# A graph layer and a routed feed-forward in one kernel: 38 blocks of routed rows pass both expert layers inside the edge gather, and the edge panels get narrower

## The chip, the cores and the metric

The kernel runs on one core of one Trainium2 chip. The metric is the device time of one execution in microseconds (us), lower is better. TensorE multiplies matrices, VectorE and ScalarE work element by element, GpSimd (POOL) here issues the gathers and scatters by indirect DMA, and SyncE (SP) issues the plain DMAs.

## The reference

```python
# _L0_gnn_ref, on mems = layernorm(x), 12500 nodes of 256 values, 200000 edges sorted by dst
mems2 = mems.at[yi].set(r[0])
_, nbr = jax.lax.top_k(-sum((mems2 - r)**2, -1), 7)         # 7 more edges into node yi
deg = segment_sum(w, col) + 2.0
dinv = rsqrt(deg)
xw = mems2 @ W
out = segment_sum((dinv[row] * w * dinv[col])[:, None] * xw[row], col)
out = out + (2.0 * dinv * dinv)[:, None] * xw
# _L0_ffn_ref, on x = layernorm(x1), 8 experts, D = 256, F = 1024
C = ceil(1.25 * T / E)                                      # T = 12500 rows, C = 1954
idx = argmax(softmax(x @ gate_w + gate_b))                  # one expert a row
pos = (cumsum(one_hot) * one_hot).sum(-1) - 1; kept = pos < C
hmid = relu(buf @ w1 + b1); ybuf = hmid @ w2 + b2           # buf: each expert's rows in order
y = nan_to_num(ybuf[idx, min(pos, C - 1)] * (prb * kept))
# the whole
x1 = x + _L0_gnn_ref(...); return x1 + _L0_ffn_ref(...)
```

dst is drawn as 12500 u^2, so that low nodes have many edges and high ones few.

## The kernel before

**Start.** VectorE derives from the edges' targets the degrees and, for each of 392 groups of 4 x 128 edges, the lowest target (`grp_base`). The scaled normalised rows are written to `z_table`. The aggregate `nodes` (256 x 12544, features on the partitions) stays in SBUF.

**Edge gather.** A turn is 8 groups (GS), and there are 49 turns, 0 to 48. For each group GpSimd issues four indirect DMAs of 128 rows of `z_table` (L561, in `gather_part`) into one of 8 slots; it may not be more than 8 groups ahead of TensorE (`agg_ps`). VectorE writes the group's one-hot panel, 4 tiles of 128 edges x 128 nodes (`select`, L1122). TensorE multiplies gathered rows and panel, 8 float32 matmuls that the trace shows as 16 records (`group`, L1645), where the gathered rows are the weights and the panel streams. VectorE adds the bank to `nodes` from the group's base on (`add_group`, L1132).

**Node blocks.** From turn Q0 = 26 on each turn also carries a block of four windows of 128 nodes that no later edge reaches: the convolution with W (`convolve`, L1672), the residual x1 (`residuals`), its norm (`variances`, `norms`, and `norm_step` on ScalarE), the transposes (L1683), the gate's logits (L1693, weights 128 x 128 and 8 columns), the softmax and choice of an expert (`gate_first`, `gate_second`), the rank among the expert's rows (`rank`, L1700 and L1701) and the row's place (`places`, from L1264). In the next turn GpSimd sends the four windows' rows (h, x1, token, gate) to their places in the DRAM table `xs` (`send`, L576). The last six windows follow after turn 48.

**Expert stage.** After the gather each of 8 experts has 8 steps of up to 256 rows (7 of 256 and one of 162). A step with no rows is skipped by an If on each engine. A step: SP loads the rows (4 slots), TensorE transposes them (L1777), VectorE copies them (L1456), TensorE makes up (L1795) and ScalarE the relu (L839), TensorE down (L1807); VectorE applies bias, gate and nan_to_num to two halves of 128 rows (L1488 to L1509), and GpSimd scatters each half into `out` (L674). For a skipped step VectorE still writes two lists of indices that point nowhere (L1516), and GpSimd still issues both scatters:

```python
dve.wait_ge(S["res_ok"], q * (2 * PC) + (2 * s + 2))
for slot in (s % 2 * 2, s % 2 * 2 + 1):
    slot_free(q, s, slot)
    nc.vector.memset(out_idx[:, slot:slot + 1], int(FAR)).then_inc(S["no_token"], 1)
```

Two experts are a pair and one pass of a loop; their weights (w1 and w2, 1 MB each an expert) lie in two buffers. Within an engine everything goes in program order, and the engines wait for each other by counting semaphores.

## Time and profile before

| | |
|---|---|
| median of 3 runs | 3101.61 us (3097.3 to 3101.98) |
| profiled execution: its time, its span | 3100.11 us, 3098.6 us |
| TensorE, VectorE, ScalarE, GpSimd busy | 2009.9, 1172.9, 457.6, 1850.6 us |
| first gather, last group of the gather ends | 172.1 us, 2293.9 us |
| first up of the expert stage | 2358.1 us |

Times are counted from the start of the span. An engine's busy time leaves out waits, branches and the issuing of DMAs by SP. A share over the whole span mixes the gather and the expert stage, and the two have different limits.

### The profile page before, as it was taken

What the parts mean: (1) busy time and instruction counts of PE and PEld (TensorE: products, weight loads), DVE (VectorE), ACT (ScalarE), POOL (GpSimd) and SP (SyncE); (2) the same over time, 40 slices, a digit from 0 to 9 for tenths busy, and PEclk for the clock granted to TensorE, in tenths of its full rate; (3) what the DMA queues carried; (4) which work ended last, traced back from release to release, by engine and by line L of the source; (5) the groups of instructions that cost most, each with busy time, mean ns of one, the idle gap of its engine ahead of it and who ended that gap; (6) DMA issues with size and microseconds to landing.
All of it is one profiled execution on the core that took longest, in us unless ns stands there. A gap on an engine that the chain in (4) does not pass through costs nothing. (4 is left out here: it accounts for less than half of the span.)

```text
span 3098.6 us, 38408 instructions
## 1 busy us (share of the span) xinstructions
PE 2009.9 (65%) x10840; PEld 1817.4 (59%) x10841; DVE 1172.9 (38%) x3705; ACT 457.6 (15%) x1152; POOL 1850.6 (60%) x1912
## 2 busy tenths in 40 slices
PE   2066555555566655666566666666655979989995
PEld 1045455555555555555555565565555868878875
DVE  8664222223212112343343343343332435434442
ACT  1341111000000000111111111111111212212221
POOL 6757777777777777777777777777741121111113
PEclk7577778777866677888887777777777989989997
DMA  9677555555444433444444444444442221222111
GB/s 234 177 223 204 154 148 146 150 150 144 142 123 130 131 104 105 130 131 138 143 130 137 143 133 134 137 129 128 136 123 97 69 77 49 68 88 78 57 59 33
DMA packets 229857, 388.32 MB, mean 125 GB/s; under 512 B 38937, under 2 KB 139967, under 8 KB 229546
## 3 DMA queue, kind: packets, MB, share of 16 engines
q0 software_dynamic: 92800, 245.57, 27.7%
q1 hardware_dynamic: 119274, 108.41, 11.8%
q10 hardware_dynamic: 17600, 32.15, 3.0%
q8 instruction: 85, 1.39, 0.2%
q14 instruction: 98, 0.80, 0.1%
HBM read 293.85 MB, written 100.43 MB: 127 GB/s over the span
## 5 line engine op out<-in xcount | busy, mean ns | idle before, releaser
L561 POOL DMA_INDIRECT arena<-z_table,arena x1568 | 1519.0, 969 | 497.5 <-issue 460.9
L1645 PE MATMUL bank<-arena 128*128 128x128 f32 x6272 | 1103.0, 349 | 805.9 <-issue 456.0
L1645 PEld LDWEIGHTS bank<-arena 128*128 128x128 f32 x6272 | 1029.8, 257 | 875.3 <-issue 609.7
L1132 DVE TENSOR_TENSOR nodes<-nodes,bank 128x256 f32 x392 | 165.1, 421 | 1336.1 <-PE bank L1645 1317.9
L674 POOL DMA_INDIRECT out<-arena x128 | 127.2, 994 | 630.1 <-DVE arena L1509 548.2
L1795 PE MATMUL bank<-arena 128*128 128x256 f32 (+1 forms) x1472 | 330.3, 384 | 24.4 <-issue 17.6
L1807 PE MATMUL bank<-arena 128*128 128x256 f32 (+1 forms) x1472 | 326.0, 379 | 0.0
L1795 PEld LDWEIGHTS bank<-arena 128*128 128x128 f32 x1472 | 282.7, 196 | 65.5 <-issue 26.9
L1807 PEld LDWEIGHTS bank<-arena 128*128 128x128 f32 (+1 forms) x1472 | 272.6, 187 | 40.1 <-issue 1.0
L1122 DVE TENSOR_TENSOR arena<-iota_b,arena 128x512 f32<-128x512 bf16 x392 | 268.6, 686 | 0.0
L839 ACT ACTIVATE arena<-bank,arena 128x256 f32<-128x256 f32 (+1 forms) x368 | 152.6, 466 | 560.2 <-PE bank L1795 560.2
L702 ACT ACTIVATE arena<-arena 128x16 int32<-128x16 int32 (+1 forms) x98 | 20.3, 210 | 790.9 <-PE bank L1645 789.9
L542 POOL DMA_INDIRECT arena<-dst_rows,first_i x98 | 100.0, 1021 | 47.4 <-issue 28.4
L576 POOL DMA_INDIRECT xs<-arena,send_idx x92 | 93.9, 1020 | 42.8 <-issue 26.5
L1456 DVE COPY arena<-bank 128x512 f32<-128x512 f32 (+1 forms) x46 | 31.2, 679 | 223.7 <-PE bank L1777 217.8
L1672 PE MATMUL bank<-arena,nodes 128*128 128x256 f32 x392 | 93.0, 391 | 0.0
L1488 DVE TENSOR_TENSOR arena<-bank,arena 128x256 f32<-128x256 f32 x92 | 39.0, 424 | 141.4 <-PE bank L1807 140.8
L745 ACT ACTIVATE arena<-arena,shift 128x256 f32<-128x256 f32 x98 | 49.1, 502 | 223.8 <-DVE arena L1139 177.5
L1672 PEld LDWEIGHTS bank<-arena,nodes 128*128 128x128 f32 x392 | 74.8, 196 | 9.5
L1590 PE MATMUL bank<-row_start,down_one 128*128 128x14 f32 (+3 forms) x10 | 3.1, 390 | 110.2 <-DVEq L934 110.2
L777 ACT ACTIVATE norm<-var 128x4 f32<-128x4 f32 (+1 forms) x24 | 4.9, 205 | 455.9 <-DVEq L1214 398.2
L1777 PE MATMUL bank<-ident,arena 128*128 128x128 f32 (+1 forms) x184 | 30.7, 288 | 57.1 <-DVEq L1529 28.2
(274 smaller groups left out, 1383.7 us busy)
## 6 DMA issues: line engine op xcount, KB each, us to landing
xs<-zeros ACTq DMA_DIRECT2D x122, 257.0 KB
arena<-z_table,arena POOLq DMA_INDIRECT x1568
arena<-xs SPq DMA_DIRECT2D x43, 514.0 KB, 4.0
arena<-in_L_ffn_w SPq DMA_DIRECT2D x16, 1024.0 KB, 7.6
arena<-in_x SPq DMA_DIRECT2D x98, 128.0 KB, 2.7
arena<-in_x SPq DMA_DIRECT2D x24, 512.0 KB, 4.2
out<-arena SPq DMA_DIRECT2D x24, 512.0 KB
nodes<-in_x SPq DMA_DIRECT2D x12, 896.0 KB, 11.9
```

The lines of the kernel that those rows point to most:

```text
L542: nc.gpsimd.indirect_dma_start(first_rows[:, h % 2, i, :], None, dst_rows, bass.IndirectOffsetOnAxis(ap=first_i[:, h * U + i:h * U + i + 1 ...
L561: nc.gpsimd.indirect_dma_start(gath[:, slot, t, :], None, z_table, bass.IndirectOffsetOnAxis(ap=idx_ring[:, half, s * GT + t:s * GT + t + ...
L576: nc.gpsimd.indirect_dma_start(xs, bass.IndirectOffsetOnAxis(ap=send_idx[:, i, s:s + 1], axis=0), h_send[:, i * BW + s, :], None, bounds_c ...
L674: nc.gpsimd.indirect_dma_start(out, bass.IndirectOffsetOnAxis(ap=out_idx[0:n, slot:slot + 1], axis=0), o_tile[0:n, slot, :], None, bounds_ ...
L745: nc.scalar.activation(sq[:, j, :], sq[:, j, :], ACT.Square, bias=shift[:, bass.ds(w, 1)], accum_out=dist[:, bass.ds(w, 1)]).then_inc(S["d ...
L839: nc.scalar.activation(hid[:, f, 0:n], up_bank[f // 2][:, f % 2 * CR:f % 2 * CR + n], ACT.Relu, bias=b1_pair[:, j * FT + f:j * FT + f + 1] ...
L1122: nc.vector.tensor_tensor(sel[:, j, :, :], iota_b[:, :].unsqueeze(1).to_broadcast([P, GT, P]), rel_b[:, bass.ds(g * GT, GT)].unsqueeze(2). ...
L1132: nc.vector.tensor_tensor(where, where, agg_bank[j][:, 0:D].rearrange("p (k c) -> p k c", k=KD), ALU.add).then_inc(S["agg_added"], 1)
L1645: last = nc.tensor.matmul(agg_bank[j][:, k * P:(k + 1) * P], gath[:, slot, t, k * P:(k + 1) * P], sel[:, j, t, :], start=(t == 0), stop=(t ...
L1672: last = nc.tensor.matmul(conv_out(j), nodes[:, k, (q - Q0) * BW + j, :], gnnw_sb[:, k, :], start=(k == 0), stop=(k == KD - 1))
L1795: last = nc.tensor.matmul(up_bank[b][:, i * CR:i * CR + n], w1_sb[:, j, k, f * P:(f + 1) * P], xs_feat[:, s % 2, k, 0:n], start=(k == 0), ...
L1807: last = nc.tensor.matmul(bank[4 + t][0:m, 0:D], hid[:, f, t * P:t * P + m], w2_sb[:, j, f, :], start=(f == 0), stop=(f == FT - 1))
```

## The change

- The node blocks begin at turn TS = 20. `TURN_OF` gives each of 23 its turn: 20 to 25, 27, 29, 31, 32, 34, 35, 37 to 40, 42 to 48. The last six windows still come after turn 48.
- From turn JT = 30 to 48 each turn carries two jobs, 38 in all. `choose` on VectorE picks, one turn ahead, the expert with the most placed rows that are not yet given out (30 small operations, 14 for each of two jobs and two more); a job with fewer than 256 rows to take works on rows of zeros behind the table. A job is a whole block: rows and weights loaded by SP, transposes, up, relu, down, results, and two scatters into `out`. It has one buffer for w1 and one for w2, in the first 32 windows of `nodes`, which are no longer needed by then.
- The expert stage keeps its 64 steps; `need_i` says which are left. Each engine reads that flag for every step, in place of the count for every pair.
- The panels are 64 nodes wide before turn 20 and 96 from there on. Three banks serve the groups from turn 20 on, four before.
- xs is zeroed by three DMAs a step instead of two, done by turn 20. Some small tensors share one block of SBUF. The way for unsorted edges (not taken with these inputs) is rebuilt to match.

```diff
+    NARROW, WIDE = 64, 96
+    WIDE_FROM = 160
+    WIDTHS = [(0, WIDE_FROM, NARROW), (WIDE_FROM, GROUPS, WIDE)]
...
-    Q0 = 26
+    TURNS = GROUPS // GS
+    TS = 20
     BW = 4
-    NB = GROUPS // GS - Q0
+    NB = 23
+    TURN_OF = []
+    for b in range(NB):
+        TURN_OF.append(max(TURN_OF[-1] + 1 if b else TS, math.ceil((GROUPS * math.sqrt((b + 1) * BW / NW) + 3) / GS)))
...
+    JT = 30
+    NJ = 2 * (TURNS - JT)
...
+        wide_bank = [bank[0], bank[1], bank[6]]
+        job_up = [bank[7], bank[5]]
...
+            def second_weights(turn):
+                k = 2 * (turn - JT)
+                e = sp.value_load(job_i[0:1, turn % 2, 1, 0:1], min_val=0, max_val=NE - 1)
+                up_done(k)
+                load_job_w1(e)
+                down_done(k)
+                load_job_w2(e, 1)
+
+            def next_first(turn):
+                k = 2 * (turn - JT)
+                sp.wait_ge(S["job_ok"], turn + 1 - JT + 1)
+                e, row = job_regs(turn + 1, 0)
+                if k >= 0:
+                    sp.wait_ge(S["res_ok"], 2 * (k + 1))
+                load_job_rows(0, row)
+                if k >= 0:
+                    up_done(k + 1)
+                load_job_w1(e)
+                if k >= 0:
+                    down_done(k + 1)
+                load_job_w2(e, 0)
...
+            for t in range(TS, TURNS):
+                if t >= JT:
+                    second_rows(t)
+                if t in BATCH_AT:
+                    store_x1(BATCH_AT[t])
+                if t >= JT:
+                    second_weights(t)
+                if t - 1 in BATCH_AT:
+                    b = BATCH_AT[t - 1]
+                    sp.wait_ge(S[f"sent{b % 2}"], 16 * BW * (b // 2 + 1))
+                    if b + 2 <= NB:
+                        load_x(b + 2)
+                if t == JT - 1:
+                    sp.wait_ge(S["conv_ps"], 32)
+                if JT <= t + 1 < TURNS:
+                    next_first(t)
...
+            def scatter_job(turn, i):
+                k = 2 * (turn - JT) + i
+                for h in range(2):
+                    pool.wait_ge(S["res_ok"], 2 * k + h + 1)
+                    nc.gpsimd.indirect_dma_start(
+                        out, bass.IndirectOffsetOnAxis(ap=out_idx[:, 2 * i + h:2 * i + h + 1], axis=0), job_out[:, 2 * i + h, :], None,
+                        bounds_check=last_node, oob_is_err=False).then_inc(S[f"out_done{2 * i + h}"], 16)
...
+                    def between(s):
+                        if t > JT and h == 0 and s == 2:
+                            scatter_job(t - 1, 0)
+                        if t > JT and h == 1 and s == 0:
+                            scatter_job(t - 1, 1)
+                        if t - 1 in BATCH_AT and h == 1 and s == 2:
+                            send(BATCH_AT[t - 1] + 1, BATCH_AT[t - 1] % 2)
...
+            def select(g, j, width=NARROW):
+                nc.vector.tensor_tensor(panel(j, width), iota_b[:, 0:width].unsqueeze(1).to_broadcast([P, GT, width]),
+                                        rel_b[:, bass.ds(g * GT, GT)].unsqueeze(2).to_broadcast([P, GT, width]),
...
+            def choose(turn):
+                then(nc.vector.tensor_scalar(count[:, :], taken_f[0:1, :], float(FULL_ROWS), None, ALU.min))
+                for i in range(2):
+                    then(nc.vector.tensor_tensor(avail[:, :], count[:, :], given[:, :], ALU.subtract))
+                    then(nc.vector.tensor_reduce(e_max[:, :], avail[:, :], AX.X, ALU.max))
...
+            def job_features(turn, i):
+                k = 2 * (turn - JT) + i
+                dve.wait_ge(S["xT_ps"], k + 1)
+                if k:
+                    dve.wait_ge(S["l1_ps"], FB2 * k)
+                nc.vector.tensor_copy(job_feat, bank[5].rearrange("p (k c) -> p k c", k=KD)).then_inc(S["xT_ok"], 1)
...
+            def job_results(turn, i):
+                k = 2 * (turn - JT) + i
+                dve.wait_ge(S["l2_ps"], 2 * k + 2)
+                for h in range(2):
+                    slot = 2 * i + h
+                    if turn > JT:
+                        dve.wait_ge(S[f"out_done{slot}"], 16 * (turn - JT))
+                    nc.vector.tensor_tensor(job_out[:, slot, :], bank[4][:, h * D:(h + 1) * D], job_b2[:, i, :], ALU.add).then_inc(S["y_ok"], 1)
+                dve.wait_ge(S["y_ok"], 2 * k + 2)
+                tokens = job_rows[:, i, :, TOK]
+                slots = slice(2 * i, 2 * i + 2)
+                then(nc.vector.tensor_scalar(out_miss[:, slots], tokens, 0.0, FAR, ALU.is_equal, ALU.mult))
+                then(nc.vector.scalar_tensor_tensor(out_f[:, slots], tokens, -1.0, out_miss[:, slots], ALU.add, ALU.add))
+                then(nc.vector.tensor_copy(out_idx[:, slots], out_f[:, slots]))
+                for h in range(2):
+                    y = job_out[:, 2 * i + h, :]
+                    token = job_rows[:, i, h, :]
+                    then(nc.vector.tensor_scalar(y, y, token[:, GATE:GATE + 1], None, ALU.mult))
+                    nc.vector.tensor_scalar(job_low, y, -BIG, -1.0e4, ALU.is_lt, ALU.mult).then_inc(S["dve_ch"], 1)
+                    nc.vector.tensor_scalar(job_high, y, BIG, 1.0e4, ALU.is_gt, ALU.mult).then_inc(S["dve_ch"], 1)
+                    ch[0] += 2
+                    then(nc.vector.tensor_scalar(job_fin, y, 0.0, 0.0, ALU.mult, ALU.is_equal))
+                    then(nc.vector.tensor_tensor(job_high, job_high, job_low, ALU.add))
+                    then(nc.vector.copy_predicated(job_high, job_fin, y))
+                    nc.vector.tensor_tensor(y, token[:, D:2 * D], job_high, ALU.add).then_inc(S["res_ok"], 1)
+                    dve.wait_ge(S["res_ok"], 2 * k + h + 1)
...
+                    g = t * GS + i
+                    add_group(g, i % SR, False, WIDE)
+                    if g + SR < GROUPS:
+                        select(g + SR, i % SR, WIDE)
+                    if i == 0 and t > JT:
+                        job_results(t - 1, 1)
                     if i == 1:
-                        if b:
-                            places(b - 1, BW)
-                        residuals(b, BW)
-                    if i == 2:
+                        if t >= JT:
+                            job_features(t, 0)
+                        if t - 1 in BATCH_AT:
+                            places(BATCH_AT[t - 1], BW)
+                        if JT <= t + 1 < TURNS:
+                            choose(t + 1)
+                        if b is not None:
+                            residuals(b, BW)
+                    if i == 2 and b is not None:
                         variances(b, BW)
-                    if i == 3:
+                    if i == 3 and b is not None:
                         norms(b, BW)
-                    if i == 6:
+                    if i == 4 and t >= JT:
+                        job_results(t, 0)
+                    if i == 5 and t >= JT:
+                        job_features(t, 1)
+                    if i == 6 and b is not None:
                         gate_first(b, BW)
-                    if i == 7:
+                    if i == 7 and b is not None:
                         gate_second(b, BW)
...
+                with dve.If(need(dve, q, s) > 0):
...
+            def turn_job(turn, i):
+                k = 2 * (turn - JT) + i
+                pe.wait_ge(S[f"xs_in{i}"], 16 * (turn - JT + 1))
+                if k:
+                    pe.wait_ge(S["hid_ok"], FT * k)
...
+            def up_job(turn, i):
+                k = 2 * (turn - JT) + i
+                pe.wait_ge(S["xT_ok"], k + 1)
+                pe.wait_ge(S["w_in0"], 16 * (k + 1))
+                for c in range(FB2):
+                    if c >= 2:
+                        pe.wait_ge(S["hid_ok"], FT * k + 2 * (c - 1))
+                    for h in range(2):
+                        f = 2 * c + h
+                        for kk in range(KD):
+                            last = nc.tensor.matmul(job_up[c % 2][:, h * CR:(h + 1) * CR], job_w1[:, kk, f * P:(f + 1) * P],
+                                                    job_feat[:, kk, :], start=(kk == 0), stop=(kk == KD - 1))
+                    last.then_inc(S["l1_ps"], 1)
...
+            def down_job(turn, i, placed):
+                k = 2 * (turn - JT) + i
+                pe.wait_ge(S["w_in1"], 32 * (k + 1))
+                pe.wait_ge(S["cnt_ok"], placed)
+                if k:
+                    pe.wait_ge(S["y_ok"], 2 * k)
...
+                        if t - 1 in BATCH_AT:
+                            rank(BATCH_AT[t - 1], BW, 2 * max(t - JT, 0))
+                        if b is not None:
+                            convolve(b, BW)
+                        if t >= JT:
+                            turn_job(t, 0)
+                    if slot == 2 and t >= JT:
+                        up_job(t, 0)
+                    if slot == 3 and t >= JT:
+                        down_job(t, 0, placed)
                     if slot == 4:
-                        turn_rows(q, i, BW, first)
-                    if slot == 5:
-                        logits(q, BW)
-            for q in range(Q0, Q0 + NB):
-                slot_turn(q, (q - Q0) % 2, q == Q0)
-            last_q = Q0 + NB
-            rank(last_q - 1, (NB - 1) % 2, BW)
-            convolve(last_q, TW)
-            turn_rows(last_q, NB % 2, TW)
-            logits(last_q, TW)
-            rank(last_q, NB % 2, TW)
+                        if b is not None:
+                            turn_rows(b, BW)
+                        if t >= JT:
+                            turn_job(t, 1)
+                    if slot == 5 and b is not None:
+                        logits(b, BW)
+                    if slot == 6 and t >= JT:
+                        up_job(t, 1)
+                    if slot == 7 and t >= JT:
+                        down_job(t, 1, placed)
```

## Rows read from the trace of the kernel before

**Rows 1.** Page, parts 1 and 2: busy us by engine; granted TensorE clock in 40 slices.

```profile
PE 2009.9 (65%) x10840; PEld 1817.4 (59%) x10841; DVE 1172.9 (38%) x3705; ACT 457.6 (15%) x1152; POOL 1850.6 (60%) x1912
...
PEclk7577778777866677888887777777777989989997
```

**Rows 2.** Groups by line: busy us, mean ns of one, idle before.

```profile
L561 POOL DMA_INDIRECT arena<-z_table,arena x1568 | 1519.0, 969 | 497.5 <-issue 460.9 <-DMA z_table<-nodes 19.8 <-PE bank L1645 13.4
...
L1795 PE MATMUL bank<-arena 128*128 128x256 f32 (+1 forms) x1472 | 330.3, 384 | 24.4 <-issue 17.6 <-DVE arena L1456 6.8
...
L674 POOL DMA_INDIRECT out<-arena x128 | 127.2, 994 | 630.1 <-DVE arena L1509 548.2 <-issue 71.0 <-DVEq L1520 10.9
```

**Rows 3.** Windows: us, busy by engine (instructions), granted clock, DMA share, GB/s.

```profile
1410.00:2294.00 884.00, 558.46 (x3289) 524.72 (x3288) 346.90 (x1256) 126.75 (x265) 668.15 (x685) 0.78 0.45 134
...
2358.00:3098.60 740.60, 666.00 (x3124) 577.01 (x3124) 317.14 (x1185) 153.29 (x371) 127.18 (x128) 0.94 0.20 63
```

**Rows 4.** Timeline, GpSimd: the first gather of turns 20, 26, 30 and 48.

```profile
989.78 1.32 POOL L561 DMA_INDIRECT arena<-z_table,arena  x1 [0.30 <-issue]
...
1232.19 0.95 POOL L561 DMA_INDIRECT arena<-z_table,arena  x1 [0.31 <-issue]
...
1410.64 0.94 POOL L561 DMA_INDIRECT arena<-z_table,arena  x1 [0.30 <-issue]
...
2241.08 0.94 POOL L561 DMA_INDIRECT arena<-z_table,arena  x1 [0.30 <-issue]
```

**Rows 5.** Timeline, TensorE: turn 30's first group and the last group.

```profile
1417.28 3.49 PE L1645 MATMUL bank<-arena 128*128 128x128 f32 x16 [3.02 <-issue]
...
2290.72 3.15 PE L1645 MATMUL bank<-arena 128*128 128x128 f32 x16 [2.61 <-issue]
```

**Rows 6.** Timeline, TensorE: groups of 128 columns and logits of 8 columns.

```profile
1722.73 0.96 PE L1693 MATMUL bank<-arena 128*128 128x8 f32 x8
...
1730.86 3.75 PE L1645 MATMUL bank<-arena 128*128 128x128 f32 x16 [6.28 <-issue]
...
1735.75 2.02 PE L1645 MATMUL bank<-arena 128*128 128x128 f32 x16 [1.13 <-issue]
...
2315.26 1.85 PE L1693 MATMUL bank<-arena 128*128 128x8 f32 x8 [0.47 <-ACT r_y L793]
```

**Rows 7.** Chain that ended last, in order of time: an expert's first blocks.

```profile
3030.06 9.83 PE bank L1795 x32
...
3040.33 6.91 PE bank L1807 x32
3047.24 6.91 PE bank L1795 x32
3054.15 0.44 PE bank L1777 x4
```

**Rows 8.** Timeline, VectorE: first and last operation of half a block's results.

```profile
2602.47 0.42 DVE L1488 TENSOR_TENSOR arena<-bank,arena 128x256 f32<-128x256 f32 x1
...
2605.53 0.42 DVE L1509 TENSOR_TENSOR arena<-arena 128x256 f32<-128x256 f32 x1
```

**Rows 9.** Timeline, VectorE: places, residuals, variances and norms of a node block.

```profile
1704.55 0.18 DVE L1264 TENSOR_TENSOR arena<-arena,bank 128x32 f32<-128x32 f32 x1
...
1707.50 1.66 DVE L1199 SCALAR_TENSOR_TENSOR arena<-bank,dinv,arena 128x256 f32<-128x256 f32 x4 [0.23 <-DVE arena L1277]
...
1710.01 1.40 DVE L1206 BATCH_NORM_STATS2 arena<-arena 128x6 f32<-128x256 f32 x4
...
1712.44 0.23 DVE L1213 SCALAR_TENSOR_TENSOR var<-gap,var 128x4 f32<-128x4 f32 x1
```

**Rows 10.** DMA issues: KB each, median us to landing.

```profile
arena<-in_L_ffn_w SPq DMA_DIRECT2D x16, 1024.0 KB, 7.6
...
nodes<-in_x SPq DMA_DIRECT2D x12, 896.0 KB, 11.9
```

**Rows 11.** Timeline, TensorE around skipped steps; GpSimd's last scatter.

```profile
2496.42 7.07 PE L1795 MATMUL bank<-arena 128*128 128x256 f32 x32
...
2528.18 2.07 PE L1795 MATMUL bank<-arena 128*128 128x256 f32 x4 [6.92 <-issue]
...
3093.67 1.10 POOL L674 DMA_INDIRECT out<-arena  x1 [0.30 <-issue]
```

More of the change, by code:

```diff
@@ L1 @@
+import math
 import concourse.bass as bass
@@ L1730, in _ @@
             with pe.If(n_bad > 0):
-                pe.wait_ge(S["rep_bad"], 1)
-                nc.tensor.matmul(bank[4][:, 0:GROUPS], ones[0:1, :], grp_bad[0:1, :], start=True, stop=True).then_inc(S["rep_dst"], 1)
+                with pe.Fori(0, NW) as w:
+                    pe.wait_ge(S["gp_in"], w * 16 + 16)
+                    for k in range(KD):
+                        last = nc.tensor.transpose(turned(0)[:, k, :], h_send[:, 0, D + k * P:D + (k + 1) * P], ident[:, :])
+                    last.then_inc(S["gp_pe"], 1)
+                pe.wait_ge(S["gp_free"], NW + 1)
                 pe.sem_inc(S["rep_free"], 1)
```

613 lines of the change are left out of this document (376 added, 237 removed).

## Prediction, made before the changed kernel ran

> **What bounds the kernel now.** I read the page first [rows 1]. TensorE is busy for 65% of the span, and its granted clock stands near 0.75 of full until about slice 29 and near 0.95 after it: two stages. The groups by line say what they are [rows 2]: 1568 row gathers on GpSimd (L561), later 1472+1472 matmuls of the expert layers, 32 and 32 a block of 256 rows, so 46 blocks. The windows [rows 3] give the sizes. From 1410 to 2294 GpSimd works 668 of 884 us and, with 0.30 us between two issues, never rests, while TensorE has 37% to spare. From 2358 to the end TensorE works 666 of 741 us. So the gather stage is bound by GpSimd's issuing, the expert stage by TensorE, and the change moves work from the second into the spare time of the first.
>
> GpSimd's turn of 8 groups comes from starts of its turns [rows 4]: turn 20 at 989.78 and 26 at 1232.19 give 40.4 us without sends; 30 at 1410.64 and 48 at 2241.08 give 46.1 us with four sends. The first matmul of turn 30 starts at 1417.28, the last group's at 2290.72 [rows 5].
>
> **What TensorE needs in such a turn.** A group is 16 records. At full clock (2.4 GHz) it takes 2.02 us, which is 0.111 us each and 1.8 us from one group to the next; at the half clock 3.75 us, or 3.4 from one to the next [rows 6]. The narrow panels shorten the streamed operand from 128 columns to 96 (64 before turn 20). The gate's matmuls with 8 columns show what that is worth: 8 records take 0.96 us at full and 1.85 us at half clock, again about 0.112 and 0.21 us each. A record with a weight load of 128 columns has this floor, so I book nothing for the narrow panels on TensorE; before turn 20 GpSimd hides TensorE anyway. The Trainium skill ("TensorE: Matmul & The Clock Gate", Back-to-back issue gap) gives for an isolated matmul a gap that falls with the columns, and says that this counts too little where weights are loaded; by the first half of it a group would take 1.3 us and not 1.8.
>
> A block costs 6.91 us up and 6.91 down plus 0.44 of transposes, 14.26 us in all [rows 7]. Two blocks and eight groups are 28.5+14.4 = 42.9 us; a node block's convolution (16 records of 0.216), transposes, logits (16 of 0.112) and ranks add some 7. That is 50 us at full clock in a turn with a node block, against GpSimd's 46.1 + 4 scatters of 1.29 (0.99 busy [rows 2] + 0.30) = 51.3. Neither alone gives the turn: the engines wait for each other in it.
>
> **The turn's chain.** VectorE does a new job's results between two groups. A half block takes 3.48 us today [rows 8]; without the small steps that are now shared, 2.65, so two halves with their bias adds are 6.7 us. The 13 small operations of places, most of them chained, take from 1704.55 to the residuals at 1707.50 [rows 9]: 0.2 us each, so the 30 of choose are 6.0 us, and places with one more 3.3. With the select at 96 columns (0.55) and the add (0.34), time 0 at the start of the turn's group 0:
> - add 0 at 2.2, select, two bias adds: y_ok at 4.1. Only then TensorE goes on with rank (0.7), convolution (3.5), transposes (0.5); group 1 starts at 8.8.
> - add 1 at 11.0, select, job_features 0.7: up(0) starts at 12.7, group 3, down(0), group 4 starts at 28.3.
> - Meanwhile VectorE: places, choose, residuals until 23.7, variances, norms until 29.5 (their lengths from [rows 9]: residuals 1.66, variances 2.7; norms are six small ones, 1.3); ScalarE's four norms end at 31.8, the node transposes 32.1, group 5 from 32.6, logits, group 6 until 38.0.
> - add 4 at 30.5, results 6.7, add 5, features: up(1) at 39.9 instead of 38.0; group 7, down(1): 55.5.
>
> So the turn is 55.5 us with a node block (15 of the 19 turns) and some 54.2 without (30, 33, 36, 41), if the clock stays full. It will not quite. TensorE has three waits of 2 to 5 us, and [rows 7] shows what follows a wait: the first up after one takes 9.83 us, 2.9 more than 6.91. Group 4 to group 6 is thin work (8-column logits and transposes between waits); I take half clock in a part of it (+1.3) and of the next up (+2), and +1.4 for the start of the turn: 60.2. The turns without node blocks wait 5 us before each up: 59.5. Ends: 55.5 with no loss; 68 with all eight groups at half clock (8 x 1.6).
>
> **The parts.**
> 1. Start: 13 more small chained VectorE operations on the bases; 0 to 4 us, taken 2. Later zeroing of xs in threes lies on ScalarE's queue behind the gather: nothing.
> 2. Turns 20 to 29: seven of them now carry sends (21 to 26, 28), before three (27 to 29): four more. 7 x 46.1 + 3 x 40.5 - (1410.64 - 989.78) = +23.
> 3. Turns 30 to 48: 15 x 60.2 + 4 x 59.5 = 1141, against 2293.9 - 1417.3 = 876.6: +264.5. Covers: GpSimd has 51 us of issuing in 60; its scatter of the second block waits until VectorE is 10 us into the next turn, which leaves it four gathered groups ahead, some 5 us of slack. SP's queue: rows, x1 store, then w1 of the second block, which must follow the store (x1_ok at 23.7) though up(0) ended at 19.6; needed at 39.9, so 15 us to land. 1 MB takes 7.6 us in the quiet stage and 0.9 MB 11.9 us at the crowded start [rows 10]; DMA would go from 134 GB/s [rows 3] to about 12 MB a turn, 200 GB/s. Taken as hidden. The other loads have 17 us or more.
> 4. Between the stages: 64 us stay; job_results ahead of places costs some 1.5.
> 5. Expert stage. I worked out the routing from the reference's inputs and followed choose(): of the 38 jobs 34 find a full block, 4 run empty; 12 of 46 blocks remain (three of them 162 rows), and 52 of 64 steps are skipped, before 18. A skip is not free: SP, TensorE and VectorE step through it, and GpSimd still issues two scatters, at least 2.6 us. Last up of an expert at 2496.42, next up at 2528.18 [rows 11]: less 14.26+3.1 for the block up to its last result, four skips and a pair's end took 14.4, 3.6 each. After the last block's result (3061.5+17.4 = 3078.9) five skips last until the end at 3098.6, 3.9 each. I take 3.0, bounds 2.6 and 3.9. Sum: 12 x 14.26 less 3 x 2.5 = 164; 8 runs of blocks, each with 3.1 to drain and 2.9 slow start = 48; 52 x 3.0 = 156; 368 in place of 744: -376. Each expert still takes 35 us or more, so its 2 MB of weights stay hidden.
>
> Sum: 2 + 23 + 264.5 + 1.5 - 376 = -85: span 3098.6 to 3013.6. The profiled execution took 3100.1, the median of the runs is 3101.6, so I add 1.5: **3015 us**, 2.8% less.
>
> **Rivals.** A measurement of this kernel tells about 0.2% (6 us) from no change.
> - Forecast, turns of 57 to 63 us: 0.42.
> - The clock stays up, turns of 55.5: 3015 - 19 x 4.7 = 2926. For it: in the expert stage clock 0.94 with shorter waits. 0.15.
> - Streamed columns count: a group would fall by 0.45 us, 3.6 a turn, 2948. This is the Trainium skill's isolated gap; the 8-column records speak against it. 0.03.
> - GpSimd is the bound (51.3): 2846. Needs chains shorter than I count. 0.05.
> - Slower: the half clock holds through all groups, turns of 68. Place: groups 4 to 7 and 0 to 2, between up and down. Price 12.8 a turn over 55.5, time 3163. For it: the granted clock is 0.78 in 1410 to 2294 [rows 3], though TensorE works 63%. Against: up and down are dense. It decides from turns of 64.7 us on (3101.6 - 3015 = 87 over 19 turns). 0.15.
> - w1 of the second block lands 5 us late, after 20 us: up(1) waits, turns of 65, 3106. For: twice the traffic. 0.15, half of it over the bound.
> - Skips at 3.9: 3062. 0.05.
>
> Slower by over 0.2%: 0.15 + half of 0.15, less what lands within: 0.20. Within 0.2%: 0.05. Faster: 0.75. Range 2920 to 3125: both clock cases' near ends and the late weights are in it; about 0.1 lies beyond each end.
>
> **What would show it.** Turn length: group 0 of turns 30 and 48 about 60 us apart each turn; 55 means no clock loss, 51 GpSimd, 65 or more a late weight load (TensorE waits for in_L_ffn_w) or half clock (groups of 3.7 us). Spacing in 96-column groups 0.112 at full clock. Turn 30 starts 25 us later than before. 12 blocks and 52 skips in about 370 us. The prediction falls if the turn is misjudged by 5 us, since 19 turns multiply it.

## The result and the profile after

The changed kernel takes 2986.17 us (median of 4 runs, 2983.49 to 2990.36); the kernel before took 3101.12 beside it. The ratio is 0.963 (95% interval 0.962 to 0.965): 3.7% faster. The forecast was 3015 us, 2.8% faster. The profiled execution has a span of 2986.1 us, 112.5 less than before.

The page, parts 1, 2 and 5, of the changed kernel:

```profile
PE 2166.6 (73%) x11158; PEld 1972.3 (66%) x11159; DVE 1186.5 (40%) x4294; ACT 477.1 (16%) x1222; POOL 1919.0 (64%) x1988
...
PEclk7575555555555666665899999998999999686777
...
L694 POOL DMA_INDIRECT arena<-z_table,arena x1568 | 1510.6, 963 | 497.3 <-issue 489.4
...
L1998 PE MATMUL bank<-arena,nodes 128*128 128x256 f32 x1216 | 310.6, 419 | 46.4 <-DVE arena L1498 46.1
...
L830 POOL DMA_INDIRECT out<-arena,early_block x128 | 126.8, 991 | 270.9 <-DVE arena L1780 153.6
```

Beside [rows 1, 2]: TensorE does the same expert work in another place. The granted clock is near full in slices 20 to 34, where the gathers and the blocks now run together, and falls in the last stage, where there is little left to do. It is also lower than before in the turns ahead of them; the section on the panel widths comes back to that. The windows of turns 30 to 48 and of the last stage (columns as in [rows 3]; the second begins 5.4 us ahead of that stage's first matmul):

```profile
1431.00:2541.00 1110.00, 997.45 (x5707) 898.30 (x5707) 614.64 (x2362) 234.88 (x558) 722.64 (x736) 0.92 0.63 198
2602.00:2986.10 384.10, 188.40 (x816) 155.55 (x816) 87.30 (x402) 39.02 (x99) 126.78 (x128) 0.74 0.19 57
```

In the turns TensorE works 90% of the time, where it had 63% in [rows 3]; GpSimd, which never rested before, now works 65%. The bound has passed from GpSimd to TensorE and its waits. Cut at the same places as the prediction's parts (the expert stage from TensorE's first transposes, at 2354.9 us before and 2607.4 after):

| part | before, us | after, us | change | predicted |
|---|---|---|---|---|
| up to GpSimd's first gather | 172.1 | 174.6 | +2.5 | +2 |
| turns 0 to 19 (GpSimd) | 817.7 | 806.7 | -11.0 | 0 |
| turns 20 to 29 (GpSimd) | 420.9 | 441.3 | +20.4 | +23 |
| GpSimd's turn 30 to TensorE's | 6.6 | 8.4 | +1.8 | 0 |
| turns 30 to 48 (TensorE) | 876.6 | 1110.5 | +233.9 | +264.5 |
| between the stages | 61.0 | 65.9 | +4.9 | +1.5 |
| expert stage | 743.7 | 378.7 | -365.0 | -376 |

One turn of the middle stage, TensorE's timeline (start, length, line, tiles, count, idle time before and its releaser), from the first group of turn 37 to the first of turn 38:

```profile
1837.70 1.92 PE L1916 MATMUL bank<-arena 128*128 128x96 f32 x16
1839.46 3.65 PE L1943 MATMUL bank<-arena,nodes 128*128 128x256 f32 x16
...
1843.38 3.71 PE L1916 MATMUL bank<-arena 128*128 128x96 f32 x32
1849.29 8.86 PE L1998 MATMUL bank<-arena,nodes 128*128 128x256 f32 x32 [2.20 <-DVE arena L1498]
1857.98 1.92 PE L1916 MATMUL bank<-arena 128*128 128x96 f32 x16
1859.74 7.10 PE L2012 MATMUL bank<-nodes,early_block 128*128 128x256 f32 x32
...
1873.24 2.48 PE L1916 MATMUL bank<-arena 128*128 128x96 f32 x16
1878.31 8.70 PE L1998 MATMUL bank<-arena,nodes 128*128 128x256 f32 x32 [2.59 <-DVE arena L1498]
1886.85 1.92 PE L1916 MATMUL bank<-arena 128*128 128x96 f32 x16
1888.60 7.10 PE L2012 MATMUL bank<-nodes,early_block 128*128 128x256 f32 x32
1895.54 1.92 PE L1916 MATMUL bank<-arena 128*128 128x96 f32 x16
```

This is the chain of the forecast. A group of 96 columns takes 1.92 us at full clock, the 128-column one 2.02 [rows 6]: at full clock the streamed columns are nearly free. Both ups of this turn wait 2 us or more for VectorE's features (L1498; 18 of the stage's 38 ups do) and take 8.7 to 8.9 us instead of 7.1, and the group ahead of the second (group 6, at 1873.24) takes 2.48; each down is full speed. The turn is 57.8 us; all turns lie between 55.7 and 60.5.

What the engines waited for in that stage (engine, tile and line, releaser: us, times, longest):

```profile
POOL out L719 <- DVE nodes L1526: 151.0, 33, 11.9
...
PE bank L1998 <- DVE arena L1498: 46.1, 18, 4.3
```

GpSimd stands 151 us ahead of the scatters of a block. There is no wait of TensorE for the weights of a block.

### The profile page after: what moved, and what is told of

The parts are those of the page before. It is cut to its first block and busy times, and to the rows that moved or that the text cites. A ratio compares the mean times of both kernels' runs of the same rounds, so it can differ in the third digit from the quotient of the medians.

```text
span 2986.1 us, 40946 instructions
## 1 busy us (share of the span) xinstructions
PE 2166.6 (73%) x11158; PEld 1972.3 (66%) x11159; DVE 1186.5 (40%) x4294; ACT 477.1 (16%) x1222; POOL 1919.0 (64%) x1988
## 5 line engine op out<-in xcount | busy, mean ns | idle before, releaser
L1916 PE MATMUL bank<-arena 128*128 128x96 f32 (+1 forms) x6272 | 1133.7, 359 | 340.4 <-issue 147.9
L1916 PEld LDWEIGHTS bank<-arena 128*128 128x128 f32 x6272 | 1096.8, 271 | 376.6 <-issue 212.0
L1316 DVE TENSOR_TENSOR nodes<-nodes,bank 128x192 f32 (+1 forms) x392 | 128.1, 327 | 1302.7 <-PE bank L1916 1255.7
L1998 PE MATMUL bank<-arena,nodes 128*128 128x256 f32 x1216 | 310.6, 419 | 46.4 <-DVE arena L1498 46.1
L1998 PEld LDWEIGHTS bank<-arena,nodes 128*128 128x128 f32 x1216 | 255.4, 213 | 91.7 <-DVE arena L1498 49.5
L2012 PE MATMUL bank<-nodes,early_block 128*128 128x256 f32 x1216 | 269.8, 380 | 0.0
L2012 PEld LDWEIGHTS bank<-nodes,early_block 128*128 128x128 f32 x1216 | 228.1, 190 | 29.4
L967 ACT ACTIVATE early_block<-bank,early_block 128x256 f32<-128x256 f32 x304 | 127.2, 469 | 587.3 <-PE bank L1998 587.1
L1305 DVE TENSOR_TENSOR arena<-iota_b,arena 128x384 f32<-128x384 bf16 (+1 forms) x392 | 195.5, 499 | 0.4 <-issue 0.3
L1943 PE MATMUL bank<-arena,nodes 128*128 128x256 f32 x392 | 110.9, 446 | 0.0
L2121 PE MATMUL bank<-arena 128*128 128x256 f32 (+1 forms) x384 | 93.9, 411 | 20.9 <-DVE arena L1729 20.9
L2121 PEld LDWEIGHTS bank<-arena 128*128 128x128 f32 x384 | 79.4, 222 | 35.0 <-issue 23.8
L1943 PEld LDWEIGHTS bank<-arena,nodes 128*128 128x128 f32 x392 | 88.0, 231 | 14.7
```

The source lines that it names most:

```text
L967: nc.scalar.activation(job_hid[:, f, :], job_up[f // 2 % 2][:, f % 2 * CR:(f % 2 + 1) * CR], ACT.Relu, bias=job_b1[:, i, f:f + 1]).then_in ...
L1305: nc.vector.tensor_tensor(panel(j, width), iota_b[:, 0:width].unsqueeze(1).to_broadcast([P, GT, width]), rel_b[:, bass.ds(g * GT, GT)].uns ...
L1316: nc.vector.tensor_tensor(where, where, held[:, 0:KD * width].rearrange("p (k c) -> p k c", k=KD), ALU.add).then_inc(S["agg_added"], 1)
L1916: last = nc.tensor.matmul(held[:, k * width:(k + 1) * width], gath[:, slot, t, k * P:(k + 1) * P], panel(j, width)[:, t, :], start=(t == 0 ...
L1943: last = nc.tensor.matmul(conv_out(j), nodes[:, k, b * BW + j, :], gnnw_sb[:, k, :], start=(k == 0), stop=(k == KD - 1))
L1998: last = nc.tensor.matmul(job_up[c % 2][:, h * CR:(h + 1) * CR], job_w1[:, kk, f * P:(f + 1) * P], job_feat[:, kk, :], start=(kk == 0), st ...
```

## The experiments

They were run on several chips of the same type, and these were of two kinds. On one kind, where the result was taken too, the kernel before takes 3101 us, on the other (three chips) 3850 to 3854; below they are the fast and the slow kind. Times are therefore compared only with kernels of the same kind, and where the kinds differ it is said. The table has them all; the segments are from the profiled executions, turns by TensorE's groups, the last stage from its first up (turns 30 to 48 here end with the last group, 7 us before the last down).

| kernel | kernel before there | time | ratio to before (95%) | turns 0-19 | 20-29 | 30-48 | last stage |
|---|---|---|---|---|---|---|---|
| before_again | 3100.7 | 3099.2 | 1.000 (0.999-1.001) | 794.9 | 421.7 | 877.1 | 739.9 |
| changed kernel | 3101.1 | 2986.2 | 0.963 (0.962-0.965) | 781.9 | 443.1 | 1103.6 | 375.6 |
| e7_panels_128 | 3100.7 | 3013.4 | 0.973 (0.971-0.975) | 783.7 | 446.8 | 1114.7 | 376.4 |
| e1_no_jobs | 3854.4 | 3815.1 | 0.989 (0.987-0.991) | 923.7 | 633.3 | 1185.1 | 745.9 |
| e2_jobs_from_40 | 3854.4 | 3793.8 | 0.983 (0.981-0.986) | 928.1 | 636.9 | 1354.0 | 554.8 |
| e3_start_panels_128 | 3854.4 | 3834.6 | 0.993 (0.990-0.996) | 934.3 | 620.3 | 1572.8 | 379.7 |
| e4_free_skips | 3854.4 | 3841.4 | 0.997 (0.995-1.000) | 935.7 | 629.6 | 1545.4 | 381.0 |
| after_again | 3852.7 | 3841.2 | 0.998 (0.996-0.999) | 922.1 | 629.9 | 1569.3 | 381.7 |
| e5_scatter_later | 3852.7 | 3760.8 | 0.976 (0.973-0.979) | 925.2 | 628.6 | 1492.2 | 379.6 |
| e9_one_look | 3852.7 | 3829.4 | 0.993 (0.990-0.995) | 942.7 | 619.1 | 1579.4 | 354.7 |
| e10_all | 3852.7 | 3714.0 | 0.963 (0.960-0.966) | 921.2 | 630.9 | 1468.7 | 351.3 |
| e10b_all | 3850.2 | 3712.7 | 0.965 (0.962-0.968) | 930.8 | 618.2 | 1470.9 | 351.3 |
| e3b_start_panels_128 | 3850.2 | 3843.5 | 0.997 (0.996-0.999) | 928.6 | 633.2 | 1572.1 | 377.3 |

**The same change on the slower kind of chip.** after_again is the changed kernel.

> The changed kernel itself, on the chip of this group of runs. If that is the chip on which the kernel before took 3854 us, every theory expects 3840 +- 15 us, as with free skips (3841) and with 128-column panels at the start (3835), since neither of these two edits showed an effect beyond 0.5%; a time below 3790 there would mean that both of them cost 50 us, and they would have to be read anew. If it is a chip on which the kernel before takes 3101 us, all expect 2986 +- 5.

3841.2 us, as expected: there the change is worth 0.25% (0.07 to 0.43), not 3.7%. before_again was to show where the kinds part.

> The kernel before itself, profiled on the chip of this run. If it is the chip on which it took 3852 us: theory A, that chip is slower where TensorE works beside GpSimd's row gathers and nowhere else, expects turns 0 to 19 at 920 to 935 us as in every kernel run there (818 on the first chip), turns 20 to 29 at 620 to 640 (421), turns 30 to 48 at 1185 to 1225, which is 310 to 350 more than the 876.6 of the first chip, and the stage from the first expert block to the end at 744 to 750 as on the first (743.7). Rival B, the chip is slower everywhere by the same share (24%), expects 920 us for that last stage. If it is a chip like the first, the profile's segments repeat within 1%.

It ran on the faster kind and repeated the first profile within 3 us in every segment, so its theories were not put to the test; the other kernels answer. The last stage takes 745.9 us without jobs on the slow kind (e1) and 739.9 on the fast, 381.7 and 375.6 with them: rival B, slower everywhere by the same share, has fallen. Turns 0 to 19 take 922 instead of 782 us, turns 30 to 48 1569 instead of 1104. So nearly all of the slow kind's loss lies where TensorE works beside the gathers; the start is longer too (188.5 instead of 174.6 us up to the first gather), the last stage by 6. TensorE's timeline in turn 39 of after_again shows how:

```profile
2557.38 2.81 PE L2012 MATMUL bank<-nodes,early_block 128*128 128x256 f32 x11
2561.24 0.46 PE L2012 MATMUL bank<-nodes,early_block 128*128 128x256 f32 x1 [1.05 <-issue]
...
2573.94 0.58 PE L2012 MATMUL bank<-nodes,early_block 128*128 128x256 f32 x1 [1.51 <-issue]
2576.04 0.58 PE L2012 MATMUL bank<-nodes,early_block 128*128 128x256 f32 x1 [1.52 <-issue]
2578.15 0.59 PE L2012 MATMUL bank<-nodes,early_block 128*128 128x256 f32 x1 [1.52 <-issue]
2580.94 0.58 PE L2012 MATMUL bank<-nodes,early_block 128*128 128x256 f32 x1 [2.21 <-issue]
...
2589.54 2.67 PE L1916 MATMUL bank<-arena 128*128 128x96 f32 x16
```

and the windows of two stretches of that turn:

```profile
2560.00:2584.00 24.00, 7.58 (x14) 3.92 (x14) 2.15 (x10) 2.33 (x4) 17.76 (x19) 0.58 0.56 185
2588.00:2600.00 12.00, 11.59 (x81) 10.98 (x79) 7.99 (x28) 3.57 (x10) 1.21 (x2) 0.78 0.47 154
```

One down (L2012) takes 32 us instead of 7.1, its matmuls starting 1.4, 2.1 or 2.8 us apart and waiting for nothing that the profile shows. In the first window GpSimd works 17.8 of 24 us and TensorE gets 14 matmuls done; in the second GpSimd rests and TensorE does 81 in 12 us. Spacings of that sort (over 0.65 us from one matmul's start to the next's, the next waiting for nothing) sum to 752 us in after_again, where the span is 853 us longer than on the fast kind, and to 1.6 us in the profiles of the fast kind. They do not come in every stretch in which GpSimd issues, but all of them save 1.6 us start within 6.4 us behind the start of an issue of GpSimd. GpSimd issues for most of the gather, so that this nearness alone proves little. Their cause is not settled.

**How much of it is the blocks' move, and what it is worth per block.** e1 sets `JT = 49` (no block moved; what follows the last turn for such blocks goes too), e2 `JT = 40`:

```
-    JT = 30
+    JT = 49        # e2: 40
```

> The changed kernel without its 38 jobs: panels of 64 and 96 and node blocks from turn 20 on stay, all 46 blocks pass in the expert stage. Theory (the gain is the jobs' alone: blocks leave the expert stage at 14.26 us less the price of a skip, and lengthen the turns 30 to 48): the expert stage goes back to about 743 us, turns 30 to 48 to 46.1 with sends and 40.3 without, 853 in all in place of 1110; 3088 us, 0.3 to 0.6% under the kernel before. Rival (the narrow panels bring a good part of the 3.7%): 3050 us or less.

> Jobs in turns 40 to 48 alone, 18 in place of 38, all with a full block. Theory (each turn with two jobs costs 13.5 us more than one without, each block moved saves 14.26 less 3.15 for its skip): 3088 + 9 x 13.5 - 18 x 11.1 + 9 = 3018 us. Rival (a job turn is long because of its start-up and its waits once, so fewer turns are cheaper in proportion, or the late turns with their node blocks are the dear ones): 3000 or less, or 3035 or more.

Both ran on the slow kind. The absolute numbers that were expected belong to the fast kind and stay untested. The last stage can be read, since the kinds agree on it: 46 blocks take 745.9 us, 28 take 554.8 and 12 take 381.7, counted by the matmuls of the ups (32 each). A block moved away is worth 191.1/18 = 10.6 us and 173.1/16 = 10.8: the trade is linear, and a block's 14.26 us [rows 7] are not all saved, 3.5 of them stay, as the price of the step that skips it and its share of the breaks between blocks. The other side of the trade is the turn. On the slow kind ten turns with jobs (30 to 39) take 808.4 us and without them 606.6, 20.2 more a turn; the 16 blocks that these turns take out of the last stage give back 17.3. On the fast kind the same ten turns went from 458.8 (before_again) to 582.6, 12.4 a turn. The two are not like for like: the kernel before has a node block and its sends in each of these turns, the changed one in seven of ten. Seven turns of 46.1 and three of 40.4 us [rows 4] make 444, if GpSimd bounded them; by this estimate the blocks themselves cost 13.9 a turn on the fast kind, against 17.3 given back. The loss in turns 30 to 39 explains 29 of the 47 us by which e2, with half of the jobs, beats all of them on the slow kind; the rest is not traced. And e1, with no job at all, is 26 us under the changed kernel there and 39 under the kernel before: on the slow kind the moved blocks cost time in sum, and what is gained comes from the rest of the change (narrow panels, node blocks from turn 20 on), which no run takes apart. On the fast kind no run leaves the jobs out; there the table of parts has +233.9 for the turns against -365.0 for the stage.

**What a skipped step costs.** e4 takes VectorE's list and its wait for a free slot out of a skipped step, and lets GpSimd, which now reads the flag too, issue the two empty scatters without waiting for VectorE (VectorE's part of the edit):

```
 with dve.Else():
-    for slot in (s % 2 * 2, s % 2 * 2 + 1):
-        slot_free(q, s, slot)
-        nc.vector.memset(out_idx[:, slot:slot + 1], int(FAR)) ...
-    dve.wait_ge(S["no_token"], ...)
```

> In a skipped step of the expert stage VectorE writes no list of indices and waits for no free slot; GpSimd issues the two scatters from a constant list that points nowhere, without waiting for VectorE. Theory (the 52 skips cost some 3.2 us each, 165 us, because they go through VectorE, GpSimd and the landing in turn; made independent, GpSimd's 2.6 us a skip lie beside the blocks' 14 us): the expert stage falls from 384 to 250-290 us, the time to 2850-2890. Rival 1 (GpSimd's own 2.6 us a skip is the price anyway): 384 - 52 x 0.6 = 353, 2955 us. Rival 2 (the rows' loads, chained through res_ok, are the price): over 2930.

The last stage is 381.0 us against 377.3 to 381.7 in after_again, e3 and e3b: nothing. My theory, that the chain through VectorE's lists makes the price, has fallen, and rival 1 with it, which had expected 353. Rival 2 had the size right, but its cause, the rows' loads, was not tested. The changed kernel's trace names another: TensorE's own sequencer takes 2.76 us from one skip to the next (2703.27 to 2706.03) without a wait. It holds two looks at the block's flag, 0.75 us each up to the branch (0.30 us of it the read), and the branches: mostly 0.1 to 0.4 us, but 15 of 148 in that stage take 0.9 to 3.7 us. The Trainium skill ("Runtime: NRT & Kernel Launch", Instruction fetch mechanics) says that a taken branch out of the prefetched pages waits for a fetch; long branches on straight skips agree with it, though no run here shows the fetch itself. e9 adds to e4 that TensorE and VectorE read each flag once a step (TensorE's part):

```
-    with pe.If(need(pe, q, s) > 0):
+    after = need(pe, q, s + 1)       # one read, used now and in the next step
+    with pe.If(flag > 0):
```

> Free skips as before, and TensorE and VectorE read the flag of each step of the expert stage once instead of twice. Theory A: a skipped step costs what TensorE's sequencer needs for it, 2.76 us from one to the next with two reads of the flag (0.30 us each, about 0.8 us with the register work and the assertion around each) and two branches; one read less makes it 1.9 to 2.0 us, 52 skips give 40 us back: ratio to the changed kernel 0.985 to 0.990, expert stage 340 to 350 us instead of 380. Rival B: the price is that of the branches or of another engine's chain (VectorE's two reads, the loads' queue, GpSimd's two scatters of 1.29 us each = 2.58 us a skip), and the stage gets shorter by less than 10 us. Both hold on either chip, because the stage took 380 us on the one and 376 us on the other.

Windows of the last stage, e4:

```profile
3447.00:3828.00 381.00, 191.12 (x812) 157.55 (x812) 81.31 (x299) 38.99 (x99) 119.05 (x120) 0.73 0.18 54
```

and e9:

```profile
3476.00:3830.00 354.00, 189.31 (x812) 156.19 (x812) 81.64 (x299) 38.57 (x99) 118.99 (x120) 0.74 0.19 58
```

The same work in 26 us less than e4 (354.7 against 381.0), 27 less than after_again. Theory A was right in kind and promised half as much again: TensorE's fastest skips went from 2.34 to 1.54 us, but branches of 0.9 us and more rose from 12 to 21 of 158, from 26.3 to 46.5 us in sum. VectorE's reads were halved by the same edit, and no run tells the two engines' shares apart. The whole kernel gained only 12 us over after_again, because its turns 0 to 48 came out 20 us longer (3141.2 against 3121.3); among the kernels in which nothing is changed that the later turns use (after_again, e3, e3b, e4, e9) they spread over 3110.7 to 3141.2 us on this kind of chip, so that only the stage itself tells such a size there.

**The wait of GpSimd.** e5 moves one line:

```
-    if t > JT and h == 1 and s == 0:
+    if t > JT and h == 1 and s == 2:
         scatter_job(t - 1, 1)
```

> One line moved: the scatters of a job turn's second block are issued two groups of gathers later (after 24 gathers of the half turn instead of before the first). Theory A: in turns 30 to 48 GpSimd stood 151.0 us in 33 waits for VectorE's result ahead of these scatters, the gathers of group 6 were issued that much later, and TensorE stood 1.7 us a turn ahead of group 6 (33 us in 19 turns); with the scatters later that goes, and some 25 us with it: 2960 against 2986, ratio to the changed kernel 0.992. Rival B: GpSimd is given back its time and TensorE's own order (work of 52.5 us a turn, waits for the choice 46 us and for the results 26 us in the stage) still sets the turn: no change within 0.3%. On the chip where the kernel before took 3854 us TensorE started every group 20 us or more behind its gathers' issue, so that both expect no change there.

Both said no change on the slow kind, and both were wrong: 3760.8 against 3841.2, 80 us, 77 of them in turns 30 to 48. The waits of that stage, after_again:

```profile
POOL out L719 <- DVE nodes L1526: 638.9, 68, 24.7
```

and e5:

```profile
POOL out L719 <- DVE nodes L1526: 479.0, 69, 16.4
...
POOL xs L709 <- DVEq L1472: 103.5, 15, 12.2
```

I had argued that TensorE starts each group 20 us or more after its gathers were issued and so can't care. But GpSimd does nothing in a turn but issue (some 47 us) and wait: 638.9/19 = 34 us of waits make up its 83, and (479.0 + 103.5)/19 = 31 its 79, near enough. In both nearly all of its waits are for VectorE's results and places, not for a slot that TensorE has yet to free. What it waits for is TensorE's second block, and TensorE crawls while it issues: there the two engines work by turns, and any wait of GpSimd that is shortened shortens the turn. That reading is argued from these rows; issue and wait must add up to the turn whatever the cause, and no run separates it. Whether e5 gains on the fast kind, where the wait is 151 us, wasn't measured.

**Panel widths.** e7 has `WIDE = 128` for 96 in turns 20 to 48 (and, for want of room, the jobs' features in another buffer); e3 and e3b have `NARROW = 128` for 64 in turns 0 to 19.

> The changed kernel with edge panels of 128 columns instead of 96 in turns 20 to 48 (64 stay in turns 0 to 19). Theory A: a group of edges takes TensorE the same (1.92 us at full clock with 96 columns, 2.02 with 128 in the kernel before) and VectorE's longer selections lie beside TensorE: within 0.5% of the changed kernel's time. Rival B: VectorE's selections are one third longer (0.56 us for 96 columns, 0.75 for 128; four more tenths of a microsecond 16 times a turn), its results and choices come later and TensorE's waits for them (46.1 and 25.7 us in turns 30 to 48) grow: +15 to +40 us, ratio to the changed kernel 1.005 to 1.013.

It ran on the fast kind: 3013.4, 27 us above the changed kernel (18 in the two profiled executions, 11 of them in turns 30 to 48). Groups by line in turns 30 to 48 of e7:

```profile
L1915 PE MATMUL bank<-arena 128*128 128x128 f32 x2416 | 308.9, 285 | 36.4 <-issue 35.3 <-DVE arena L1304 0.9
...
L1304 DVE TENSOR_TENSOR arena<-iota_b,arena 128x512 f32<-128x512 bf16 x148 | 101.4, 685 | 0.0
L1315 DVE TENSOR_TENSOR nodes<-nodes,bank 128x256 f32 x151 | 63.3, 419 | 404.8 <-PE bank L1915 368.7 <-DVE nodes L1525 19.2 <-issue 10.4
```

and of the changed kernel:

```profile
L1916 PE MATMUL bank<-arena 128*128 128x96 f32 x2434 | 308.1, 284 | 36.4 <-issue 35.1 <-DVE arena L1305 1.3
...
L1305 DVE TENSOR_TENSOR arena<-iota_b,arena 128x384 f32<-128x384 bf16 x149 | 82.8, 556 | 0.0
L1316 DVE TENSOR_TENSOR nodes<-nodes,bank 128x192 f32 x153 | 54.0, 353 | 424.1 <-PE bank L1916 386.5 <-DVE nodes L1526 16.7 <-issue 14.2
```

TensorE's mean is 285 ns with 128 columns and 284 with 96: in these turns nothing, as the prediction booked. VectorE's selection takes 685 instead of 556 ns and its addition 419 instead of 353, eight of each a turn, 1.6 us; and VectorE is on the turn's chain: up(0) starts 0.8 us later in the turn and up(1) 1.0. Rival B is borne out in sign and size.

What neither theory had is the granted clock. Windows of turns 20 to 29 (from 988) and 30 to 48, e7:

```profile
988.00:1440.00 452.00, 279.57 (x1668) 258.76 (x1668) 167.22 (x588) 52.25 (x116) 344.77 (x353) 0.79 0.45 136
1440.00:2560.00 1120.00, 997.05 (x5690) 895.21 (x5691) 642.60 (x2355) 233.94 (x556) 724.26 (x734) 0.94 0.62 196
```

the changed kernel (turns 0 to 19, then 20 to 29):

```profile
174.00:981.00 807.00, 608.50 (x2763) 576.26 (x2761) 183.49 (x538) 87.54 (x316) 611.39 (x641) 0.52 0.56 162
988.00:1431.00 443.00, 323.48 (x1642) 303.21 (x1643) 146.06 (x569) 52.11 (x114) 336.68 (x350) 0.63 0.46 138
```

and turns 0 to 19 of the kernel before, with panels of 128:

```profile
172.00:985.00 813.00, 476.93 (x2745) 435.81 (x2743) 243.91 (x535) 86.79 (x315) 618.70 (x638) 0.76 0.55 156
```

With 96 columns the granted clock of turns 20 to 29 is 0.63, with 128 it is 0.79; with 64 in turns 0 to 19 it is 0.52 instead of 0.76, and TensorE is busy 132 us longer with the same groups. So narrow panels are free on TensorE at full clock, but in turns 0 to 29 the clock granted to it fell with the width. It cost no time there, since GpSimd bounds those turns; where TensorE is the bound it would have to be counted.

> The changed kernel with panels of 128 nodes before turn 20, 96 after. Theory A (the shorter select on VectorE holds up GpSimd's issuing less; turns 0 to 19 took 806.7 us in place of 817.7): they go back to about 817, the whole to 2997 us. Theory B (the 11 us come from something else, such as the moved start): no change, 2986 within 3 us. In both the TensorE groups before turn 20 keep their spacing at either clock, and with 128 columns the clock rises again to about 0.75 there, which moves no time since GpSimd is the bound.

> The changed kernel with edge panels of 128 columns instead of 64 in turns 0 to 19. On a chip of the first kind: turns 0 to 19 took 794 to 795 us in two profiles of the kernel before (panels of 128) and 782 and 784 in two with panels of 64. Theory A, the panels make this difference (VectorE and TensorE free a panel earlier, so GpSimd waits less): turns 0 to 19 go back to 793 to 796 and the time rises by 8 to 12 us to 2994 to 2998. Rival B, it comes from something else that the change moved (its other buffers and queues): 2986 +- 4.

Both landed on the slow kind, where turns 0 to 19 of kernels with 64 columns spread over 921 to 943 us; with 128 they took 934.3 and 928.6. No effect on the time can be seen there, and the 11 us of the fast kind stay unexplained by a run. The granted clock of these turns was 0.66 in both, and 0.50 with 64 columns in after_again: it goes with the width there too.

**All together.** e10 and e10b are one kernel: e4, e9, e5, and ranking and the convolution with W behind edge group 1 of a turn with jobs instead of group 0 (`if slot == (1 if t >= JT else 0):`).

> Free skips, one look at each flag, scatters of the second block later, and ranking and first-layer product behind the second edge group of a job turn instead of the first (so that the results of the block before are ready when TensorE asks for them: 25.7 us of waits in 14 turns). Theory A: the terms add up: -40 (looks), -25 (scatters), up to -20 (results), so 2905 to 2930 where the kernel before takes 3101, and -40 alone where it takes 3854 (3800). Rival B: in the turns nothing is won, and the time is that of the one-look run within 0.3% on either chip.

> The same kernel as before (free skips, one look, later scatters, later convolution), if possible on a chip of the first kind. On the chip where the kernel before takes 3852 us its expert stage was 30 us shorter (351.3 against 381.7) and turns 30 to 48 were 100 us shorter (1469 against 1569). Theory A: on the first kind of chip the stage gives the same 28 us, and the turns give back what GpSimd and TensorE waited for there, no more: 15 to 45 of the 105 us (58.4 us a turn against 52.5 of work on TensorE); 2915 to 2945 us, ratio to the kernel before 0.940 to 0.950. Rival B: the turns are set by TensorE's order and only the stage gives: 2958 +- 5.

Both fell on the slow kind: 3714.0 and 3712.7, 127 to 129 us under the changed kernel there (0.967 of it) and 3.7 and 3.5% under the kernel before. The last stage gave 30 us, turns 30 to 48 98 to 101, of which e5 alone had given 77. Theory A of e10 had expected 40 us here and nothing from the turns, so its sum was 87 of 127 us too small; 77 of them are e5's, and the other 22 us or so of the turns came with the later ranking and convolution, which no run has alone. e10b's theories were for the fast kind and stay untested. It beats both kernels on this kind of chip; on the fast kind it has not been timed.

## Why the prediction was right

The sign, the mechanism and the range held. The forecast of the profiled span (3013.6 us) was 27.5 us too long, made of parts that partly cancel:

- **Turns 30 to 48, +233.9 for +264.5.** The chain was right to a microsecond or so in its places: mean starts after group 0 are 12.3 for up(0) (12.7 predicted), 28.5 for group 4 (28.3), 30.6 for the node transposes (they were to end at 32.1), 41.2 for up(1) (39.9). What was mis-sized is the clock loss, booked at 4.7 us a turn. The turn is 58.4 us for 60.2 and 59.5, some 3 over the chain at full clock. The granted clock is 0.92. Group 6, behind the gate's logits, takes 2.0 to 3.7 us, 0.9 a turn over full clock; the other seven groups are at full clock. The ups take 8.2 us in the mean instead of 7.1, 2.2 us a turn, and the convolutions 0.5. The rival in which the half clock holds through all groups is refuted by seven groups of 1.92 to 2.00 us.
- **GpSimd's slack.** I gave it 5 us before its late scatter would starve TensorE. It waited 151 us, up to 11.9 at once, and TensorE stood 35.1 us in 10 of the 19 turns ahead of group 6, 6.4 at most. So a part of what the clock gave was taken back by late gathers, which the chain had at nothing. Turn 30, ahead of whose gathers no block's scatter stands, has such a wait too (5.9 us), so the scatters are not all of its cause.
- **Weights hidden.** w1 and w2 of the moved blocks landed in a median of 5.9 us at 198 GB/s, with no wait of TensorE for them. The rival of late weights did not occur.
- **Expert stage, -365.0 for -376.** 12 blocks and 52 skips came as worked out. What was mis-sized is the skip, booked at 3.0 us although the prediction's own rows gave 3.6 and 3.9. The breaks between the runs of blocks, with the tail, are 196 us for 52 skips and eight drains; less 3.1 for each drain that is 3.3 a skip, some 16 us more than booked. The first blocks of a run gave a part back: they lost less to the clock than the 2.9 us that were booked for each.
- **Narrow panels.** Nothing on TensorE is right for turns 30 to 48 (284 and 285 ns), but not for the turns before, where the granted clock fell from 0.76 to 0.52 in turns 0 to 19 and to 0.63 in turns 20 to 29. It did no harm because GpSimd bounds them; the prediction had that reason for turns 0 to 19 only. VectorE's gain stood in my chain (0.55 and 0.34 us); e7 shows that it is worth 18 to 27 us.
- **Turns 20 to 29, +20.4 for +23**, four more turns with sends. **Start and gap between the stages:** +2.5 for +2 and +4.9 for +1.5.
- **Not foreseen:** 11 us less in turns 0 to 19. With 128 columns they took 794 to 795 us in both profiles, with 64 columns 782 and 784 (changed kernel and e7). The narrow panels are the likeliest cause; the run that would show it fell on the other kind of chip.

What no part of the prediction held is the chip. On the slow kind the same kernel gains 0.25%, because a turn with two blocks pays 20.2 us there for the 17.3 that it takes out of the last stage. That the forecast met a chip of the fast kind, as the profile it was made from, was luck.

## What to carry to other kernels

Filling one engine's idle time under another's bound is a trade per unit: what the unit costs in the new place (here an estimated 13.9 us a turn for two on one kind of chip, 20.2 measured on the other) against what it gives back when it is gone from the old one (10.7 of its 14.3 us, because the skipped step and the breaks between blocks stay). Price a skip from the sequencer's records, reads of flags and branches first; one read less a step on TensorE and VectorE was worth 26 us here, and taking out its work nothing. And where engines hand work to each other within a turn, moving one line of an idle-looking engine can be worth more than the other edits together: 77 us in the turns of the slow kind, where the whole change had given 11.

## What the runs showed of the hardware

- Two kinds of chips: 3101 and 3852 us for one kernel, within 6 us in the last stage (381.7 and 375.6 us for the changed kernel), 18% apart in turns 0 to 19 and 42% in turns 30 to 48 with blocks. Matmuls that wait for nothing start over 0.65 us apart there, often 1.4 to 2.8, for 752 us in sum.
- A scatter whose indices are all out of bounds occupies GpSimd as long as a full one (990 ns against 996 in e9, and 1.29 us from one to the next).
- A read of a flag from SBUF into a register costs TensorE's sequencer 0.30 us, and a branch mostly 0.1 to 0.4 us and up to 3.7 (15 of 148 take 0.9 or more); no branch of VectorE in that stage took over 0.07 us.
- Records with a 128-column weight load follow each other as fast with 96 as with 128 streamed columns at full clock (284 and 285 ns busy each, overlapping).
- Fewer streamed columns can lower the granted clock: 0.79 with panels of 128 columns, 0.63 with 96 (turns 20 to 29, e7 and changed kernel); 0.76 with 128, 0.52 with 64 (turns 0 to 19, kernel before and changed kernel).
